# A one-core attention and mixture-of-experts kernel: the order of its front end is changed

## The reference

```python
q = relu(queries @ Wq_w.T + Wq_b); k = relu(keys @ Wk_w.T + Wk_b); v = relu(values @ Wv_w.T + Wv_b)
attn = softmax(einsum('bhsd,bhtd->bhst', qh, kh) / sqrt(8))
a = transpose(einsum('bhst,bhtd->bhsd', attn, vh), (0, 1, 3, 2)).reshape(q.shape)
return a + queries
```

## Time and profile before

| what | us |
|---|---|
| three runs | 664.58, 668.88, 671.4 (median 668.88) |
| the profiled execution, its own time | 670.79 |
| its span | 669.0 |
| busy in the span: PE, DVE, ACT, POOL | 532.2, 539.4, 429.6, 229.0 |
| start of slot 0 (first `score_columns`) | 72.20 |
| a transfer of 1 MB of w1 or w2, issue to landing, median | 5.9 |
| SyncE's issue of 3 rows of in_proj_b, 4 of b2, 6 other rows | 5.32, 2.56, 2.72 |

### The profile page before, as it was taken

The page is one execution under the profiler, slowest core; times in us unless marked ns, Lnnn a source line. Parts: engine busy times, 40 slices in busy tenths (PEclk is TensorE's granted clock), DMA queues, the critical chain, the costliest instruction groups (busy, mean ns, idle before and its releaser), DMA issues.

```text
span 669.0 us, 9878 instructions
## 1 busy us (share of the span) xinstructions
PE 532.2 (80%) x3439; PEld 212.6 (32%) x3439; DVE 539.4 (81%) x867; ACT 429.6 (64%) x914; POOL 229.0 (34%) x360
## 2 busy tenths in 40 slices
PE   2884799999999998999999988476587685998710
PEld 1550122222222222222222215355467542443300
DVE  4969699999999998999999800988838156899996
ACT  2550489998898888988889885134344404566554
POOL 7001000000034440354403650662344401676761
PEclk9995599999999999999999999688687775999955
DMA  9832010111111111201221002000000000000112
GB/s 243 255 136 106 14 37 23 40 33 46 54 60 30 34 53 47 65 26 32 59 57 49 8 9 62 15 1 1 0 1 1 1 1 0 0 1 0 32 31 63
DMA packets 31285, 28.92 MB, mean 43 GB/s; under 512 B 6132, under 2 KB 23676, under 8 KB 31236
## 3 DMA queue, kind: packets, MB, share of 16 engines
q1 hardware_dynamic: 29204, 27.31, 13.8%
q10 hardware_dynamic: 2032, 0.98, 0.6%
HBM read 19.23 MB, written 8.65 MB: 42 GB/s over the span
## 4 chain that ended last, share of the span: by engine, by line
PE 38%; DVE 27%; POOL 15%; ACT 8%; issue 8%; DMA 3%; SPq 1%; ACTq 0%; DVEq 0%; POOLq 0%
PE ps L1267 11%; PE ps L1262 8%; DVE row_max L1436 8%; PE ps L1235 4%; PE ps L593 3%; DVE space L872 2%; DVE st L241 2%; POOL space L382 2%; POOL space L384 2%; POOL smallp L379 2%; ACT attended L1384 1%; DMA space<-max_turned 1%; PE ps L578 1%; DVE space L863 1%; DVE space L264 1%
## 5 line engine op out<-in xcount | busy, mean ns | idle before, releaser
L1436 DVE TENSOR_REDUCE row_max<-ps 128x2 f32<-128x1024 f32 x256 | 299.7, 1219 | 20.2 <-PE ps L1235 17.3
L1368 ACT ACTIVATE space<-ps 128x512 f32<-128x512 f32 x512 | 271.9, 605 | 45.0 <-PE ps L1262 44.5
L1262 PE MATMUL ps<-space 51*128 51x512 bf16 x512 | 159.5, 388 | 9.6 <-DMA space<-max_turned 5.8
L1267 PE MATMUL ps<-space 128*32 128x512 f32 x1024 | 138.1, 612 | 3.0 <-ACT space L1368 0.7
L1235 PE MATMUL ps<-space 48*128 48x512 bf16 x512 | 128.8, 401 | 14.2 <-DVE row_max L1436 12.5
L1137 POOL CAST max_parts<-row_max 128x16 bf16<-128x16 f32 x32 | 6.3, 197 | 269.9 <-DVE row_max L1436 269.9
L1262 PEld LDWEIGHTS ps<-space 51*128 51x128 bf16 x512 | 41.2, 94 | 170.9 <-ACT space L1368 149.1
L593 PE MATMUL ps<-W,space 128*128 128x512 f32 x128 | 72.0, 646 | 0.0
L428 POOL TENSOR_TENSOR space<-PC,same_row 128x512 f32<-128x512 f32 x32 | 32.8, 1057 | 62.9 <-DVE PC L768 62.9
L710 ACT ACTIVATE space<-ps,weight 128x128 f32<-128x128 f32 x128 | 34.3, 383 | 21.2 <-PE ps L593 9.5
L1235 PEld LDWEIGHTS ps<-space 48*128 48x128 bf16 x512 | 26.6, 94 | 54.9 <-DVE row_max L1436 49.1
(11 more groups left out here) (192 smaller groups left out, 701.0 us busy)
## 6 DMA issues: line engine op xcount, KB each, us to landing
q_parts_dram<-space SPq DMA_DIRECT2D x2, 1536.0 KB, 5.5
space<-q_parts_dram SPq DMA_DIRECT2D x64, 48.0 KB
attended_dram<-attended SPq DMA_DIRECT2D x128, 18.0 KB
X<-in_L_attn_queries SPq DMA_DIRECT2D x8, 256.0 KB, 7.7
space<-in_L_ffn_w SPq DMA_DIRECT2D x2, 1024.0 KB, 5.9
space<-q_parts_dram SPq DMA_DIRECT2D x64, 32.0 KB
space<-attended_dram SPq DMA_DIRECT2D x16, 128.0 KB, 2.4
space<-inverses_dram SPq DMA_DIRECT2D x16, 128.0 KB
```

The source lines that it names most:

```text
L1262: pe.matmul(ps[:, col_bank(v), :], k_rows[rows_a, kappa // 4 % 2, tc * P:(tc + 1) * P], q_stack[rows_a, kappa % 4, b * S:(b + 1) * S], sta ...
L1267: mm = pe.matmul(ps[32 * m:32 * m + 32, PV, :], v_heads[:, tc, PAIR * (kappa // 4) + m % PAIR, :], probs[:, tc % 2, m, :], start=(tc == 0) ...
L1368: act.activation(probs[:, tc % 2, m, :], ps[:, col_bank(v), :], ACT.Exp, scale=1.0 / math.sqrt(DH)).then_inc(s_pr, 1)
L1436: dve.tensor_reduce(row_max[:, par].rearrange("p (a c) -> p a c", a=PAIR)[:, :, item], ring(n), AX.X, MAX).then_inc(s_free, 1)
```

## The change

The front end is put into another order, engine by engine; the slots and the back end are left as they are.

- SyncE loads units 0 and 1 of x first, and units 2 and 3 once the attention's weights, keys and values are there. The k parts are stored by three DMAs that read a part several times, in place of six; the keys are loaded ahead of the first store of q. The second half of w1 and w2 and the small rows are loaded behind the first two stacks; the second store of q stands behind the first `load_shift`.
- Two units are normed together: both variances, then both applications, with buffers of their own. The inverse square root is GpSimd's power with exponent -0.5, in place of ScalarE's root and VectorE's reciprocal. GpSimd's first two powers stand ahead of its memsets and of the 15 selects that make `same_row`.
- Three weight tiles are turned at first, and the other four behind the projection of batches 0 to 3.
- VectorE splits the q of batches 0 to 3 ahead of the norm of units 2 and 3, and that of batches 4 to 7 between the eight reductions of slot 0 and the eight of slot 1. `c_row` comes behind all 16.
- Batches 4 to 7 are turned and projected one by one between the row items of slot 0, in two banks; the second half of the fold runs between the row items of slot 1.

The diff, cut to its core (`-` before, `+` after; the line in front of a part names the engine):

```diff
 @@ -78 +78 @@
-        k_dram = nc.dram_tensor("k_rows_dram", (NH, KROWS, S), BF16, kind="Internal").ap()
+        k_dram = nc.dram_tensor("k_rows_dram", (NH, DH, len(PRODUCTS), S), BF16, kind="Internal").ap()
+        def raise_to_minus_half(pool, k, small):
+            pool.wait_ge(s_var, k + 1)
+            pool.tensor_tensor(small[:, 3, :], small[:, 2, :], neg_half[:], ALU.pow).then_inc(s_sd, 1)
+        q_bank = lambda b: b if b < QB else 6 + b % 2
-        def fold_weights(pe, r):
+        def fold_weights(pe, r, between=lambda j: None):
...
                 mm.then_inc(s_wu, 1)
+                between(j)
...
-                if e == 5:
-                    root(act, 3)
 SyncE
+            load_unit(0)
+            load_unit(1)
...
+            sp.wait_ge(s_w, 16 * 3)
+            sp.wait_ge(s_kv, 32)
+            load_unit(2)
+            load_unit(3)
...
             load_weights(0)
-            for j in range(3):
-                sp.dma_start(bias_col[:, 3 + j:4 + j], bin_[...]).then_inc(s_bin, 16)
-            load_weights(1)
             sp.wait_ge(s_ks, 1)
-            for r, (_, part) in enumerate(PRODUCTS):
-                sp.dma_start(k_dram[:, r * DH:(r + 1) * DH, :].rearrange("h d t -> h d t"),
-                             k_parts[:, part, :]).then_inc(s_kst, 16)
-            sp.wait_ge(s_const, 5)
...
+            for part, first, times in ((0, 0, 3), (1, 3, 2), (2, 5, 1)):
+                sp.dma_start(k_dram.rearrange("h d r t -> (h d) r t")[:, first:first + times, :],
+                             k_parts[:, part:part + 1, :].broadcast_to([P, times, S])).then_inc(s_kst, 16)
+            def load_rest():
...
+            sp.wait_ge(s_kst, 16 * PARTS)
+            sp.wait_ge(s_const, 5)
+            load_keys(0)
             store_q(0)
-            sp.wait_ge(s_kst, 16 * len(PRODUCTS))
-            sp.wait_ge(s_const, 6)
-            load_keys(0)
             sp.wait_ge(s_qst[0], 16)
             load_stack(0)
             load_stack(1)
+            load_weights(1)
+            load_rest()
+            sp.wait_ge(s_pr, 1)
+            load_shift(0)
             store_q(1)
             sp.wait_ge(s_qst[1], 16)
             load_stack(2)
+            sp.wait_ge(s_const, 6)
             sp.wait_ge(s_csplit, 1)
...
-            sp.wait_ge(s_pr, 1)
-            load_shift(0)
 GpSimd
             pool.tensor_copy(ident16[:], ident[:]).then_inc(s_const, 1)
+            raise_to_minus_half(pool, 0, small)
+            raise_to_minus_half(pool, 1, smallp)
...
+            raise_to_minus_half(pool, 2, small)
+            raise_to_minus_half(pool, 3, smallp)
             split_max(8, 0)
 TensorE
-            pe.wait_ge(s_w, 16 * 5)
-            for j in range(7):
+            pe.wait_ge(s_w, 16 * 3)
+            for j in range(3):
...
+            def turn_batch(b):
+                pe.wait_ge(s_xn, 4)
+                if b >= QB + 2:
+                    pe.wait_ge(s_qe, b - 1)
+                for g in range(G):
+                    mm = pe.transpose(ps[:, q_bank(b), g * P:(g + 1) * P], XN[:, g, b, :], ident[:])
+                mm.then_inc(s_xt, 1)
+            def project_batch(b):
...
             turn_unit(0)
             turn_unit(1)
-            project_half(0)
+            for b in range(QB):
+                project_batch(b)
+            pe.wait_ge(s_vpe, 1)
+            pe.wait_ge(s_win, 32)
+            for j in range(4):
+                mm = pe.transpose(ps[:, 5, j * P:(j + 1) * P], w_in[:, 3 + j, :], ident[:])
...
             fold_weights(pe, 0)
-            pe.wait_ge(s_qe, QB)
-            turn_unit(2)
-            fold_weights(pe, 1)
-            turn_unit(3)
-            project_half(1)
+            pe.wait_ge(s_Wc, 1)
+            turn_batch(QB)
             pe.wait_ge(s_kl[0], 32)
             pe.wait_ge(s_ql[0], 96)
+            pe.wait_ge(s_qe, QB)
+            score_rows(0, 0, 0)
+            score_rows(1, 0, 1)
+            for b in range(QB, B):
+                project_batch(b)
+                if b + 1 < B:
+                    turn_batch(b + 1)
+                    for item in (2 * (b - QB) + 2, 2 * (b - QB) + 3):
+                        score_rows(item, 0, item)
+            turn_max(0)
             pe.wait_ge(s_qe, B)
-            for item in range(8):
-                score_rows(item, 0, item)
             pe.wait_ge(s_ql[1], 96)
-            for item in range(8):
-                if item == 4:
-                    pe.wait_ge(s_Wc, 2)
-                    pe.wait_ge(s_csum, 1)
-                    turn_max(0)
-                score_rows(8 + item, 1, item)
+            def rows_of_second_slot(j):
+                for item in (2 * j, 2 * j + 1):
+                    score_rows(8 + item, 1, item)
+            fold_weights(pe, 1, rows_of_second_slot)
+            pe.wait_ge(s_Wc, 2)
+            pe.wait_ge(s_csum, 1)
             pe.wait_ge(s_vb, TC)
 ScalarE
-            root(act, 0)
...
+            for b in range(QB):
+                copy_batch(b)
+                if b:
+                    project_q(act, b - 1)
+            project_q(act, QB - 1)
+            act.wait_ge(s_wt, 2)
+            act.copy(wT[:, 3:7].rearrange("p j f -> p (j f)"), ps[:, 5, :]).then_inc(s_wtc, 1)
+            copy_weights(act, 0)
+            copy_folded(act, 0)
+            copy_batch(QB)
+            for b in range(QB, B):
+                if b + 1 < B:
+                    copy_batch(b + 1)
+                project_q(act, b)
+            copy_turned(0)
+            copy_weights(act, 1)
+            copy_folded(act, 1)
...
-            copy_turned(0)
             exps(0, 0)
 VectorE
-            norm_unit(0)
-            norm_unit(1)
+            def norm_units(first):
+                both = ((first, st6, small), (first + 1, st6p, smallp))
+                for u, stats, scale in both:
+                    dve.wait_ge(s_x[u], 32)
+                    norm_variance(dve, ch, at(X, u), stats, scale)
+                for u, stats, scale in both:
+                    dve.wait_ge(s_sd, u + 1)
+                    norm_apply(dve, at(X, u), at(XN, u), scale).then_inc(s_xn, 1)
+            norm_units(0)
...
+            for b in range(QB):
+                split_q(b)
+            norm_units(2)
             dve.wait_ge(s_vpe, 1)
             dve.wait_ge(s_vset, 2)
...
-            norm_unit(2)
-            for b in range(QB):
-                split_q(b)
-            norm_unit(3)
-            for b in range(QB, B):
-                split_q(b)
...
             for item in range(8):
                 reduce_rows(item, 0, item)
+            for b in range(QB, B):
+                split_q(b)
+            for item in range(8):
+                reduce_rows(8 + item, 1, item)
             dve.wait_ge(s_bw, 2)
...
-            for item in range(8):
-                reduce_rows(8 + item, 1, item)
```

More of the change, by code:

```diff
@@ L965, in _, with load_unit @@
         def _(sp):
-            for u, unit in enumerate(UNITS):
-                for g, b in (unit[0], unit[QB]):
+            def load_unit(u):
+                for g, b in (UNITS[u][0], UNITS[u][QB]):
                     sp.dma_start(X[:, g, b:b + QB], x_tok[g][:, b:b + QB]).then_inc(s_x[u], 16)
+            load_unit(0)
+            load_unit(1)
             for j, row in enumerate((bq, bk, bv)):
@@ L1183, in _ @@
             pe.wait_ge(s_const, 4)
-            pe.wait_ge(s_w, 16 * 5)
-            for j in range(7):
-                mm = pe.transpose(ps[:, 4 + j // 4, (j % 4) * P:(j % 4 + 1) * P], w_in[:, j, :], ident[:])
+            pe.wait_ge(s_w, 16 * 3)
+            for j in range(3):
+                mm = pe.transpose(ps[:, 4, j * P:(j + 1) * P], w_in[:, j, :], ident[:])
             mm.then_inc(s_wt, 1)
@@ L1206, in turn_unit @@
                 for g, b in UNITS[u]:
[L1207 removed]
+                    mm = pe.transpose(ps[:, b, g * P:(g + 1) * P], XN[:, g, b, :], ident[:])
                 mm.then_inc(s_xt, 1)
[L1210 to L1213 removed]
+            def turn_batch(b):
[6 more added lines that the diff above has]
+            def project_batch(b):
+                pe.wait_ge(s_xtc, b + 1)
+                pe.matmul(ps[:, q_bank(b), :], wT[:, 0, :], featT[:, b, :], start=True, stop=True).then_inc(s_qp, 1)
             turn_unit(0)
             turn_unit(1)
[L1217 removed]
+            for b in range(QB):
[4 more added lines that the diff above has]
+                mm = pe.transpose(ps[:, 5, j * P:(j + 1) * P], w_in[:, 3 + j, :], ident[:])
+            mm.then_inc(s_wt, 1)
             pe.wait_ge(s_kpe, 1)
[L1219 removed]
             pe.wait_ge(s_b1, 16)
             turn_b1(pe)
+            pe.wait_ge(s_wtc, 2)
             fold_weights(pe, 0)
[L1223 to L1227 removed]
             def score_rows(n, kappa, item):
@@ L1335, in _ @@
             act.activation(k_rest[:, 0], ps[:, 4, :], ACT.Relu, bias=bias_col[:, 1:2]).then_inc(s_kpe, 1)
-            def project_half(half):
-                act.wait_ge(s_xt, 2 * (half + 1))
-                for b in range(QB * half, QB * half + QB):
```

(35 more changed lines are left out.)

40 lines of the change are left out of this document (15 added, 25 removed).

## The result

Fifteen runs of the changed kernel have a median of 673.49 us (668.13 to 676.91), fifteen of the kernel before 669.28 (664.58 to 679.92). The ratio is 1.008, with a 95% interval of 1.0053 to 1.0106. The profiled execution of the changed kernel took 674.71 (span 672.9), 3.92 more than that of before.

What follows compares the result with a forecast made beforehand. Slot 0's start was taken as bound by VectorE's list and the turned maxima's DMA arriving together; summed along VectorE's list it moved from 72.2 to 69.0, 3.2 us off the 668.88 median: 665.7, range 660.5 to 671.5.

Steps and rivals of the forecast that it cites:

- The diff touches no slot: Slots: taken as untouched, so the change is worth the earlier start of slot 0 plus its effect on that slot.
- What costs nothing: Front end: GpSimd's delayed memsets and selects, held-back loads and three k stores all stay covered, at no cost.
- GpSimd beside VectorE: First q splits: GpSimd's selects beside them slow VectorE by 0.5 us, bounds 0 and 3.1.
- Units 0 and 1: First norms on VectorE: unit 1 lands at 8.7, both applications end at 15.8 against 19.08 before.
- The early clock: Batches 0 to 3: TensorE's early projections and turns may run at half rate; 1.0 us allowed, first copy at 18.2.
- First stack: From the first q store at 29.0, the stack is there at 40.5; the first reduction starts at 41.0.
- Sixteen items: Row items of slots 0 and 1: eight reductions end at 51.5, splits 58.7, eight more 67.8; 1.4 us extra allowed.
- SyncE past the start: Slot 0: third stack costs 0.4 us; slot 1's shift lands at 80.4, wanted at 81.2, late if slot 0 is fast.
- Rival 3: Front end: TensorE becomes the bound, at half clock after its pause; start 75 to 77, time 672 to 674; chance 0.12.
- Rival 2: Front end: gain eaten by selects or cold-start turns of units 0 and 1; gain 0 to 0.7, about 668.5; chance 0.2.
- The power: Norm: GpSimd's power, 1.67 us against 0.2 + 0.2 for roots, is no faster; the order brings the gain.

Runs made afterwards that it cites:

- (1): Changed kernel with k's DRAM layout, six stores and one-run key loads as before; against the kernel before: median 668.87 us, ratio 0.9993.
- (2): Kernel before with only the new k layout, its three stores and permuted loads; against the kernel before: median 673.0 us, ratio 1.0064.
- (3): Changed kernel with GpSimd's seven memsets ahead of its first two powers; against the kernel before: median 670.49 us, ratio 1.0024.
- (5): Changed kernel with the old k layout and GpSimd's memsets ahead of its powers; against the kernel before: median 667.66 us, ratio 0.9972.
- (6): Changed kernel, old k layout, memsets ahead of powers, bias row's four DMAs moved behind slot 2's shift; against the kernel before: median 666.0 us, ratio 0.9957.
- (7): Repeat of the kernel with old k layout, memsets first and bias row's DMAs behind slot 2's shift; against the kernel before: 666.77 us, ratio 0.9951.
- (10): Changed kernel, old k layout, bias row's DMAs later, ScalarE's root and VectorE's reciprocal replacing GpSimd's power; against the kernel before: 667.05 us, ratio 0.9973.

## Why the prediction was wrong, by its steps

*"The diff touches no slot."* This failed, and it cost 4.6 us of runs by (1), up to 4.0 by (2). `load_keys` runs in every fourth slot; the edit to its source pattern stood in the whole diff. I counted the bytes and the cover of the first load, and not what the seven later ones cost SyncE, nor who is queued behind them. Of the changes to that transfer I had written "the same bytes as six".

*"What costs nothing": GpSimd's memsets.* This failed for 3.0 us (3). I asked who wants what the memsets make, and not what runs beside them. They now ran beside VectorE's applications. I allowed 0.5 for GpSimd beside VectorE, for the selects and the splits, in another place. There the size was 0.3: the four splits took 31.09 - 23.66 = 7.43, against 7.16. The upper bound of 3.1 did not come, since it was GpSimd that took longer: the fifteen selects took 8.38 in all, in place of 6.60, and a subtraction of two tiles on VectorE at most 0.78, in place of 0.69. The Trainium skill, "SBUF — State Buffer", section "Who interferes with whom", which I had cited for instructions with two inputs, says in the same list that a `tensor_scalar` can enter a mode in which it and a GpSimd instruction exclude each other. The trace agrees for the memsets (1.918 beside 1.85); for the power (1.75 long, eight elements wide) it doesn't: 0.34 each beside it.

*Units 0 and 1.* Unit 1 of x was waited for until 9.43, where I took 8.7: 0.7 of size, and in the other kernels with this order it came between 8.85 and 10.35. With the 2.9 of the memsets it ends at 19.38, not 15.8.

*The early clock.* The allowance of 1.0 was not needed in the changed kernel. The projections of k and v and the turns of unit 0 did run at half rate, but under the slowed applications: the first copy came 1.18 behind unit 1.

```profile
13.09 2.05 PE L1217 MATMUL ps<-space,wT 128*128 128x512 f32 x2 [1.19 <-ACT space L1369]
14.93 1.92 PE L1219 MATMUL ps<-wT,space 128*128 128x128 f32 x8
16.64 1.91 PE L1227 MATMUL ps<-ident,XN 128*128 128x128 f32 x8
19.43 0.77 PE L1227 MATMUL ps<-ident,XN 128*128 128x128 f32 x5 [0.88 <-DVE XN L269]
```

With the norm fast it was needed, and about right: in (3), (5), (6) and (7) the copy came 2.1, 3.0, 2.5 and 2.9 behind unit 1, against 1.39 before, so 0.7 to 1.6 more.

*First stack.* The store went out at 31.12 in place of 29.0, and the first reduction at 43.84 in place of 41.0. The store and the six loads took what was said; the other 0.7 is the first items and turns at half clock (1.04 for four matmuls, and the earlier trace rows for the level).

*Sixteen items.* The first eight took 10.9, where 10.5 was said, the last eight 9.7 for 9.4. The sizes held. So did the splits, and the start of slot 0 came 3.5 late, which is the 2.8 of the first reduction and these.

*SyncE past the start.* Right as a wait: slot 1's shift was late by 1.27 once slot 0 was not all at half clock, and (6) and (7) take it away. What it is worth in time isn't shown.

*The rivals.* None was this one. Rival 3 had the sign, and even the size (672 to 674), but by luck, for its place was wrong: TensorE's pause came and the clock fell for 6.8 us, not until slot 0, and slot 0 started at 72.11 and not at 75 to 77. Rival 2's size for the start (0 to 0.7 gained) was met by another cause. What was missing is a rival in the slots.

*The power.* The prediction had said that the order counts and not the power. That was right: the power was hidden, and (10) shows the roots only 0.45 later.

What stays open: the 1.8 us by which (1) and (3) together give less than their sum, though the profile of (5) against that of (3) shows how: 1.2 by the early clock, which differs from one execution to the next; how many of the runs of (2) lost their time in that way; how much of the half clock ahead of batch 4 is paid.

## What to carry to other kernels

A change of layout is paid at each reader, in issue time of its queue, and the price is set by what is queued behind it there: here three slots of seven paid, those whose shift was late already. Count the loads inside the loop before the one ahead of it. When work that "nobody wants early" is moved, ask what it will run beside. When a diff seems to stop at a border (here slot 0), check each helper that both sides call.

## What the runs showed of the hardware

- The issue of a DMA of 48 rows of 1 KB took SyncE 0.32 to 0.42 us (from the third pair of loads on) when its source was one run, and 0.71 to 0.87 (all 16 of the changed kernel) when the same rows were read in another order of two dimensions. The bytes were the same.
- A VectorE subtraction and multiplication of 128x128 float32 with scalar columns, 0.34 by itself, took 1.92 us beside a GpSimd memset of 1.85; beside GpSimd's power on 128x8 (1.75) and beside its selects it took 0.33 to 0.42.
- TensorE's first work ran at half rate in every profiled execution, for a time that differed though the instructions up to there were the same: in the kernel before the projection of k took 1.10 at 16.70, and with only the k layout changed 2.05 at 16.77. It made 2.0 us at the start of slot 0 (72.20 and 74.17).
- GpSimd's split of 128x16 maxima took 2.4 us beside VectorE's splits of q, and 1.05 with VectorE at reductions (from 74.45). The slow one:

```profile
54.79 0.59 POOL L1155 CAST max_parts<-row_max 128x16 bf16<-128x16 f32 x1 [16.73 <-DVE row_max L1479]
55.46 0.40 POOL L1157 TENSOR_TENSOR max_rest<-row_max,max_parts 128x16 f32<-128x16 f32 x1
55.92 0.65 POOL L1159 CAST max_parts<-max_rest 128x16 bf16<-128x16 f32 x1
56.65 0.54 POOL L1161 TENSOR_TENSOR max_parts<-max_rest,max_parts 128x16 bf16<-128x16 f32 x1
```

- The granted clock fell to 1.2 GHz behind a pause of 2.04 us in slot 9, where it had not behind 1.28; the slot grew by 2.0 for 0.8 of pause. The length alone doesn't decide: behind 1.60 in slot 25 it fell, behind 1.86 in slot 17 it did not.
